# One more pair of key blocks joined in the softmax sums of an attention and MLP block, and two transposes moved behind other matmuls

## The chip, the cores and the metric

The kernel runs on one core of a Trainium2 chip. The metric is the device time of one execution in microseconds (us); the median of three executions of the kernel before is 3200.17 us, from 3200.02 to 3200.99.

## The reference

The input x has 8 sequences of 1024 rows and 512 columns. All arithmetic is float32. A condition vector per sequence gives six modulation vectors: shift, scale and gate for the attention half and for the MLP half.

```
mod = silu(condition) @ Wada + bada          # sh_a, sc_a, gt_a, sh_m, sc_m, gt_m
xm  = layernorm(x, g1, be1) * (1 + sc_a) + sh_a
q, k, v = split(xm @ Wqkv)                   # 16 heads of 32
scores = q k^T * 32**-0.5, masked to k <= q  # causal
x   = x + gt_a * ((softmax(scores) v) @ Wproj + bproj)
xm  = layernorm(x, g2, be2) * (1 + sc_m) + sh_m
x   = x + gt_m * (gelu(xm @ W1 + b1) @ W2 + b2)
```

## The kernel before, in words

Large products are made of three matmuls each, high by high, low by high and high by low part, so that the reduced float32 format of TensorE gives nearly full precision.

The attention is cut into 32 items: one sequence and four heads each. An item is worked through in 20 steps (`score_chunks`), two steps to a slot. A step is one block of 128 keys against a quarter (256) of the queries that may see it; the quarters come last to first, so an item's slots are 0 to 3 (last quarter), 4 to 6, 7 and 8 (second quarter), and 9 (first quarter). Slots 3, 6, 8 and 9 (`DIAG_SLOTS`) hold the diagonal blocks: their first 128 columns are masked after the exponential, and the second of their two blocks is only 128 queries wide.

Two items make a body of 40 steps, s = 0 to 39. There are 16 bodies. In the first 13 (`with_a`) TensorE also does, between the steps, the projections q, k, v of rows further ahead (`a_item`, twelve to a body); in the first 12 of these (`with_ln`) a block of x is also normalised and transposed (`a_turn`, L742, one per 128 columns, four to a body, at the steps of `TURN_AT`: 23, 29, 33, 35). The last three bodies have neither. A stage after them does projection and MLP, and is not touched.

Every engine runs its own list of instructions in order, written out by hand, and waits on semaphores. In a step of a body with `with_a` TensorE (PE) does: the scores of the step in two halves (L838); a transpose of x if the step has one (L756); its share of a projection (L784, L788), unless a new one starts at an odd step, which then comes last (`late`); a piece of the bound on the maximum of a later item, if the step has one (`max_item`, L807; VectorE reduces it at L1345, `max_reduced`); and at odd steps the sums over keys of an earlier slot (`added_sums`, L849), the products with v of the slot before (`values`, L876), and that slot's sums if it is a diagonal one (`diagonal_sums`, L893 and L898). ScalarE does the exponentials (L1097, tile `e`, a ring of 8 steps) and copies each finished projection out of PSUM (L1087), after which `a_turn` may write into that bank, and modulates the transposed block (L1074), after which the next projection may.

The denominators are sums over keys, made by matmuls with a matrix of ones. To have fewer of them GpSimd (POOL) first adds blocks to each other. `SUM_GROUPS[True]` says which slots share one place in the ring `es` of two: before, (0,1,2), (3), (4,5), (6), (7), (8), (9). The first slot of a group is one addition of its two blocks (L1663). A further slot is two: `half_add` (L1639) adds the slot's first block to the place, and then `add` (L1656) adds the second. For a diagonal slot alone, L1663 adds the two halves that are 128 wide, and `diagonal_sums` sums the other 128 columns of `e` itself (L893) and the 128 added ones (L898). It waits for the semaphore `added` between the two, and PE's next instructions are the scores of the step after. POOL also masks the diagonal blocks (L1626), splits q and k into high and low parts (`a_low`, L1617) and takes the power for the normalisation at step 15 (L1610). `values` waits for both masks of its slot.

Of the kernel before, what the change touches and what calls it, by code (L numbers as in the profile page):

```python
# [24 lines left out]
SLOTS = NCH // 2  # L25
# [8 lines left out]
AHEAD = 3  # L34
# [17 lines left out]
TURN_AT, TURN_AFTER = (23, 29, 33, 35), (7, 9, 10, 11)  # L52
# [81 lines left out]
def placed(chunks):  # L134

    return [(*chunk, sum(c[3] for c in chunks[:n])) for n, chunk in enumerate(chunks)]
# [3 lines left out]
DIAG = [c for c, (_, kt, q0, _) in enumerate(CHUNKS) if q0 == P * kt]  # L140


DIAG_SLOTS = [i for i in range(SLOTS) if 2 * i in DIAG]
OTHER_SLOTS = [i for i in range(SLOTS) if i not in DIAG_SLOTS]

SUM_GROUPS = {True: [(0, 1, 2), (3,), (4, 5)] + [(i,) for i in range(6, SLOTS)], False: [(i,) for i in range(SLOTS)]}

HALF_ADDED = [i for g in SUM_GROUPS[True] for i in g[1:]]
HALF_ADDS = len(HALF_ADDED)


def sum_place(h, i, with_a):

    groups = SUM_GROUPS[with_a]
    n = next(n for n, g in enumerate(groups) if i in g)
# [3 lines left out]

SUMS_END = {with_a: [g[-1] for g in groups] for with_a, groups in SUM_GROUPS.items()}  # L160
assert all({groups[-2][-1], groups[-1][-1]} <= set(DIAG_SLOTS) and groups[-1] == (9,) for groups in SUM_GROUPS.values())
LAST_SLOT = {CHUNKS[2 * i][0]: i for i in DIAG_SLOTS}
# [5 lines left out]
def item_at(s):  # L168

    for n, shares in enumerate(A_SHARES):  # L170
        if s < len(shares):
            return n, sum(shares[:s]), sum(shares[:s + 1])
        s -= len(shares)
    return None
# [13 lines left out]
def wait(eng, sem, value):  # L188

    if isinstance(value, int) and value <= 0:  # L190
        return
    eng.wait_ge(sem, value)


def build(nc, x, cond, Wqkv, Wproj, bproj, W1, b1, W2, b2, g1, be1, g2, be2, Wada, bada, out):
# [26 lines left out]
    with ExitStack() as keep:  # L222
        sems = {}

        def sem(name):
            if name not in sems:
                sems[name] = keep.enter_context(nc.semaphore(name))
            return sems[name]
# [477 lines left out]
        def _(pe):  # L706
# [87 lines left out]
            def max_item(u, ahead, n, masks):  # L794

                i = u * 2 + ahead
                if n == 0:  # L800
                    pe.wait_ge(max_loaded[ahead % 2], (u + ahead // 2 + 1) * 32)
                    wait(pe, sem("m_turned"), i)
                wait(pe, sem("max_reduced"), i * NMX + n)
                for qt, part, k0, w, col in placed(MAXES[n][0]):
                    for h in range(GH):
                        rows = slice(HD * h, HD * (h + 1))
                        mm = pe.matmul(psS[:, h, col:col + w], qmx[rows, ahead % 2, qt * P:(qt + 1) * P],  # L807
                                       kmx[rows, ahead % 2, k0:k0 + w], start=True, stop=True,
                                       skip_group_check=True)
                chunks, diag = MAXES[n]  # L810
                if masks and diag is not None:
                    for h in range(GH):
                        at = psS[:, h].rearrange("p (j c) -> p j c", c=P)[:, diag]
                        mm = pe.matmul(at, ident_b[:], mask_b[:].to_broadcast([P, len(chunks) if diag.step else 1, P]),
                                       start=False, stop=True, skip_group_check=True)
                mm.then_inc(sem("max_formed"), 1)
# [25 lines left out]
            def added_sums(u, t, with_a):  # L842

                h, i = divmod(t, SLOTS)
                place, slots, _ = sum_place(h, i, with_a)
                pe.wait_ge(sem("added"), (u * 2 + h) * SLOTS + i + 1)
                past(pe, "pe")
                for hd in range(GH):
                    mm = pe.matmul(psO[HD * hd:HD * (hd + 1), QUART:2 * QUART], ones[:],  # L849
                                   es[:, place, hd, :], start=False, stop=True,  # L850
                                   skip_group_check=True)
                mm.then_inc(sem("summed"), len(slots))
# [65 lines left out]
            def body(u, with_a, with_ln):  # L918
                last = isinstance(u, int) and u == NU - 1
                for s in range(BODY_STEPS):  # L920
                    h, r = divmod(s, NCH)
                    ahead = u == 0 and s == 0
                    if ahead:
                        a_item(AHEAD, *item_at(0), False, with_ln)


                    slot = s % 2 == 1 and not (u == 0 and s == 1)
                    between = s % 2 == 1 and not with_a
                    piece = MAX_AT.get(r)
                    if piece and last and h + piece[0] >= 2:  # L930
                        piece = None
                    sums = slot and s // 2 >= 2 and (s // 2 - 2) % SLOTS in [i for i in SUMS_END[with_a] if i not in DIAG_SLOTS]
                    scores(u, s, 0, with_a)
                    if between and piece:
                        max_item(u, h + piece[0], piece[1], True)
                    elif between and sums:
                        added_sums(u, s // 2 - 2, with_a)
                    scores(u, s, 1, with_a)
                    if with_ln and s in TURN_AT[:-1]:
                        a_turn(u + AHEAD + 1, TURN_AT.index(s), False)  # L940
                    at = item_at(s) if with_a else None
                    late = s % 2 == 1 and at is not None and at[1] == 0
                    if at and not late and not ahead:
                        a_item(u + AHEAD, *at, False, with_ln)
                    if r == MAX_TURN_AT and not (last and h == 1):
                        max_turn(u, h + 1)
                    if piece and not between:
                        max_item(u, h + piece[0], piece[1], not with_a)
                    if slot:
                        t = s // 2  # L950
                        if sums and (piece or not between):
                            added_sums(u, t - 2, with_a)
                        values(u, t - 1)
                        if with_ln and s == TURN_AT[-1]:
                            a_turn(u + AHEAD + 1, A_TURNS - 1, False)
                        diagonal_sums(u, t - 1)
                    if late:
                        a_item(u + AHEAD, *at, False, with_ln)
                    if last and s in FIRST_PROJECT_AT:
                        project(0, 0, FIRST_PROJECT_AT.index(s))  # L960
# [3 lines left out]
            for ia in range(AHEAD):  # L964
                for n in range(A_ITEMS):
# [9 lines left out]
                    if (ia, n) in MAX_ALONE_AT:  # L975
                        ahead, piece = MAX_ALONE_AT[ia, n]
# [10 lines left out]
            for u in range(1, NU - AHEAD - 1):  # L987
                body(u, True, True)
# [597 lines left out]
        def _(pool):  # L1586
# [42 lines left out]
            def half_add(u, t, with_a):  # L1629

                h, i = divmod(t, SLOTS)
                place, slots, _ = sum_place(h, i, with_a)
                if i != slots[0]:
                    if i in DIAG_SLOTS:
                        pool.wait_ge(sem("masked"), (u * 2 + h) * len(DIAG) + 2 * DIAG_SLOTS.index(i) + 1)
                    else:
                        pool.wait_ge(sem("exp_done"), (u * BODY_STEPS + 2 * t + 1) * 2)
                    pool.wait_ge(sem("added"), u * BODY_SLOTS + t)
                    pool.tensor_tensor(es[:, place], es[:, place], e[:, 2 * t % ERING], ALU.add)\  # L1639
                        .then_inc(sem("half_added"), 1)  # L1640
# [35 lines left out]
            def body(u, with_a, with_ln, after_a, pieces):  # L1676
                for s in range(BODY_STEPS):
                    mask(u, s)
                    if s % 2 == 0:
                        half_add(u, s // 2, with_a)  # L1680
                    else:
                        add(u, s // 2, with_a)
                    item = formed(u, s, 1, LOW_LATE, with_a, after_a)
                    if item:
                        a_low(*item)
                    if with_ln and s == LN_AGGR_AT:
                        a_rstd(u + AHEAD + 1)
                    if isinstance(u, int) and u == NU - 1 and s == FIRST_RSTD_AT:
                        rstd_2(0)
                    for part in range(2):  # L1690
                        q = PIECE_AT.get(s - PIECE_LOW_LAG - 2 * part)
                        if q is not None and q < pieces:
                            piece_low(u, q, part)
# [76 lines left out]
```

## Time and profile before

| | us |
|---|---|
| median of three executions | 3200.17 |
| the profiled execution | 3200.24 |
| its span, first to last instruction | 3198.5 |
| PE busy in it | 3129.8 |
| DVE (VectorE) busy | 2351.6 |
| POOL (GpSimd) busy | 1742.8 |
| ACT (ScalarE) busy | 1189.0 |

The span is 1.74 us shorter than the profiled execution's own time. The 13 bodies that the change touches lie between about 173 and 1359 us of the span, and twelve of them take about 92.9 us each; the last stage begins at about 1573 us. All times in rows are from the span's start. Busy time is that in which an engine had an instruction running; a PE that is always busy still waits now and then for a part of a microsecond between rows, which is seen as a jump of the start times.

### The profile page before, as it was taken

How to read it: one execution, taken by the hardware profiler on the slowest of the kernel's cores; microseconds unless marked ns; L12 is line 12 of the kernel's file. 1: busy time of each engine (PE TensorE's matmuls, PEld its weight loads, DVE VectorE, ACT ScalarE, POOL GpSimd, SP SyncE). 2: the span in 40 equal slices, each digit the busy share in tenths (PEclk: the TensorE clock that was granted, in tenths of full speed). 3: DMA queues.
4: the chain of work that ended last, by engine and by line, in shares of the span. 5: the costliest groups of instructions: out<-in, count | busy, mean ns of one | idle time of the engine just before them, and what ended most of it. 6: DMA issues, size and time to landing. Idle time of an engine off the chain costs nothing.

```text
span 3198.5 us, 68318 instructions
## 1 busy us (share of the span) xinstructions
PE 3129.8 (98%) x24936; PEld 2522.6 (79%) x24936; DVE 2351.6 (74%) x2981; ACT 1189.0 (37%) x2354; POOL 1742.8 (54%) x1385
## 2 busy tenths in 40 slices
PE   7999999999999999999899999999999999999999
PEld 5667777776777777766688888989898898988888
DVE  4678887787888777766777767677777777777673
ACT  3355555555555555566521212112121121212211
POOL 3288887888888878888743333233332333333232
PEclk9999999999999999999999999999999999999999
DMA  6666666666656665676612222121322212122120
GB/s 240 215 179 188 177 188 184 176 182 181 195 171 190 185 181 165 193 194 167 167 40 80 48 70 71 47 79 41 77 58 60 79 39 79 54 64 72 46 66 14
DMA packets 304611, 391.85 MB, mean 123 GB/s; under 512 B 24280, under 2 KB 206072, under 8 KB 304432
## 3 DMA queue, kind: packets, MB, share of 16 engines
q1 hardware_dynamic: 292320, 371.86, 40.9%
q10 hardware_dynamic: 12112, 17.42, 1.6%
q8 instruction: 135, 2.21, 0.3%
q14 instruction: 44, 0.36, 0.0%
HBM read 270.66 MB, written 118.00 MB: 122 GB/s over the span
## 4 chain that ended last, share of the span: by engine, by line
PE 89%; DVE 5%; issue 2%; ACT 2%; DMA 1%; POOL 1%; SPq 0%; DVEq 0%; ACTq 0%; POOLq 0%
PE psH L1009 23%; PE psY L1022 22%; PE psA L784 9%; PE psT L838 8%; PE psA L876 8%; PE psP L913 6%; PE psA L788 5%; PE psS L807 4%; DVE mx L1345 2%; PE psA L849 2%; PE psA L756 1%; DVE psS L1341 1%; PE psA L898 1%; ACT e L1097 1%; PE psA L893 1%
## 5 line engine op out<-in xcount | busy, mean ns | idle before, releaser
L1605 POOL TENSOR_TENSOR h_l<-h_full,h_h 128x256 fp32r<-128x256 f32 x512 | 489.8, 957 | 1080.6 <-DVE h_h L1518 1080.6
L1097 ACT ACTIVATE e<-psT 128x512 f32<-128x512 f32 (+1 forms) x1202 | 606.0, 554 | 531.5 <-PE psT L838 529.0
L1345 DVE TENSOR_REDUCE mx<-psS 128x4 f32<-128x2048 f32 (+3 forms) x384 | 665.8, 1755 | 116.7 <-PE psS L807 79.5
L1220 ACT ACTIVATE h_full<-psH,b1c 128x256 f32<-128x256 f32 x512 | 242.9, 475 | 1226.9 <-PE psH L1009 1226.9
L1009 PE MATMUL psH<-a_h,w1p_h 128*128 128x256 f32 x2048 | 575.2, 281 | 2.2 <-DVE a_l L1513 2.2
L1009 PE MATMUL psH<-a_l,w1p_h 128*128 128x256 f32 x2048 | 577.0, 282 | 0.0
L1009 PE MATMUL psH<-a_h,w1p_l 128*128 128x256 f32 x2048 | 576.7, 282 | 0.0
L1663 POOL TENSOR_TENSOR es<-e 128x512 f32<-128x512 f32 (+1 forms) x242 | 446.3, 1845 | 168.6 <-ACT e L1097 83.9
L1518 DVE CAST h_h<-h_full 128x256 fp32r<-128x256 f32 x512 | 180.8, 353 | 404.1 <-ACT h_full L1220 401.2
L838 PEld LDWEIGHTS psT<-qst,kst 97*128 97x128 f32 x2404 | 349.1, 189 | 114.4 <-issue 70.8
L838 PE MATMUL psT<-qst,kst 97*128 97x256 f32 (+1 forms) x2404 | 410.4, 290 | 4.5 <-ACT e L1097 3.3
L1009 PEld LDWEIGHTS psH<-a_h,w1p_h 128*128 128x128 f32 x2048 | 388.3, 190 | 24.6 <-DVE a_l L1513 2.6
L1009 PEld LDWEIGHTS psH<-a_l,w1p_h 128*128 128x128 f32 x2048 | 388.9, 190 | 21.7
L1022 PE MATMUL psY<-w_l,h_h 128*128 128x512 f32 x1024 | 404.6, 395 | 0.0
L1022 PE MATMUL psY<-w_h,h_h 128*128 128x512 f32 x1024 | 402.0, 393 | 2.5 <-DVE tmp L1525 2.5
L1022 PE MATMUL psY<-w_h,h_l 128*128 128x512 f32 x1024 | 402.6, 393 | 0.0
L1009 PEld LDWEIGHTS psH<-a_h,w1p_l 128*128 128x128 f32 x2048 | 389.5, 190 | 0.0
L876 PE MATMUL psA<-e,vst 128*32 128x256 f32 (+1 forms) x5120 | 313.7, 362 | 9.3 <-ACT o_sb L1105 7.3
L1431 DVE RECIPROCAL oin<-oin 128x256 f32<-128x256 f32 x128 | 221.9, 1739 | 47.0 <-DMA oin<-sums 47.0
L876 PEld LDWEIGHTS psA<-e,vst 128*32 128x32 f32 x5120 | 146.0, 109 | 122.4 <-issue 45.0
L1617 POOL TENSOR_TENSOR qk_hl<-qk_hl 128x512 fp32r<-128x512 f32 x128 | 166.8, 1304 | 122.1 <-ACT qk_hl L1180 68.8
L1495 DVE STREAM_TRANSPOSE a_full<-xc 32x256 f32<-32x256 f32 x512 | 223.3, 436 | 9.4
(118 smaller groups left out, 5213.5 us busy)
## 6 DMA issues: line engine op xcount, KB each, us to landing
qk_split<-qk_hl SPq DMA_DIRECT2D x128, 512.0 KB, 3.6
kst<-qk_split SPq DMA_DIRECT2D x128, 256.0 KB, 3.9
qst<-qk_split SPq DMA_DIRECT2D x128, 256.0 KB, 4.2
xin<-in_x_dram SPq DMA_DIRECT2D x64, 256.0 KB, 3.5
values<-vout ACTq DMA_DIRECT2D x64, 256.0 KB, 3.3
kmx<-qk_split SPq DMA_DIRECT2D x32, 512.0 KB, 4.7
qmx<-qk_split SPq DMA_DIRECT2D x32, 512.0 KB, 5.7
kst<-qk_split SPq DMA_DIRECT2D x128, 128.0 KB, 3.8
```

Source lines behind the costliest of these rows:

```text
L784: mm = pe.matmul(psA[:, bank, :], w[:, k, m * P:(m + 1) * P], a[:, k, :], **ends)
L838: mm = pe.matmul(bank[:, d, 0:w], kst[0:97, hd, key_cols(kt, h)], qst[0:97, q0 // HALF, hd, q0 % HALF:q0 % HALF + w], start=True, stop=Tru ...
L876: mm = pe.matmul(psO[HD * hd:HD * (hd + 1), c:c + w], vst[:, h, kt, HD * hd:HD * (hd + 1)], e[:, (2 * t + d) % ERING, hd, 0:w], start=(kt ...
L1009: mm = pe.matmul(psH[:, m % 4, 0:RA], w[:, k, m * P:(m + 1) * P], a[par][:, k, :], start=(n == 0), stop=(n == 3 * KT - 1))
L1022: mm = pe.matmul(psY[:, r, :], a[:, m % 4, r * P:(r + 1) * P], w[:, w2_at(m), :], start=(m == 0 and n == 0), stop=(m == FT - 1 and n == 2) ...
L1097: act.activation(e[:, s % ERING, 2 * hp:2 * hp + 2, 0:w], score_bank(s, hp, with_a)[:, :, 0:w], ACT.Exp, scale=SCALE).then_inc(sem("exp_do ...
L1220: act.activation(h_full[:, m % 4, :], psH[:, m % 4, 0:RA], ACT.Gelu, bias=b1c[:, m:m + 1])\
L1345: reduce = dve.tensor_reduce(mx[:, part, :, qt], psS[:, :, col:col + w], AX_X, ALU.max)
L1431: dve.reciprocal(oin[:, 1, k], oin[:, 1, k]).then_inc(sem("sums_inverted"), 1)
L1495: t = dve.transpose(cols[:, :, :, a], rows[:, :, :, b])
L1605: return pool.tensor_tensor(dst, full, high.bitcast(F32), ALU.subtract)
L1663: pool.tensor_tensor(to, first, second, ALU.add).then_inc(sem("added"), 1)
```

## The change

One more group of two slots: (7) and (8) become (7,8). Slot 8 is diagonal, so three rules change with it. `half_add` of a diagonal slot is issued at the odd step, after both masks of the slot and just ahead of its `add`, and waits for both masks. `added_sums` no longer sums slot 7, and `diagonal_sums` of slot 8 takes all 256 columns from `es` after the `added` of slot 8, with no matmul on `e`. The lists without projections (the last three bodies) stay as they are. On PE, the transposes at steps 23 and 29, where a piece of the maximum falls too, are issued behind that piece; those at 33 and 35 stay.

```diff
-SUM_GROUPS = {True: [(0, 1, 2), (3,), (4, 5)] + [(i,) for i in range(6, SLOTS)], False: [(i,) for i in range(SLOTS)]}
+SUM_GROUPS = {True: [(0, 1, 2), (3,), (4, 5), (6,), (7, 8), (9,)], False: [(i,) for i in range(SLOTS)]}
@@ TensorE, body
-                    if with_ln and s in TURN_AT[:-1]:
+                    turn = with_ln and s in TURN_AT[:-1]
+                    if turn and not piece:
                         a_turn(u + AHEAD + 1, TURN_AT.index(s), False)
...
                     if piece and not between:
                         max_item(u, h + piece[0], piece[1], not with_a)
+                    if turn and piece:
+                        a_turn(u + AHEAD + 1, TURN_AT.index(s), False)
@@ GpSimd, half_add
-                        pool.wait_ge(sem("masked"), (u * 2 + h) * len(DIAG) + 2 * DIAG_SLOTS.index(i) + 1)
+                        pool.wait_ge(sem("masked"), (u * 2 + h) * len(DIAG) + 2 * DIAG_SLOTS.index(i) + 2)
@@ GpSimd, body
                     mask(u, s)
-                    if s % 2 == 0:
+                    if (s % 2 == 1) == (s // 2 % SLOTS in DIAG_SLOTS):
                         half_add(u, s // 2, with_a)
-                    else:
+                    if s % 2 == 1:
                         add(u, s // 2, with_a)
```

## Rows read from the trace of the kernel before

**Rows 1.** The page: busy time by engine.
```profile
PE 3129.8 (98%) x24936; PEld 2522.6 (79%) x24936; DVE 2351.6 (74%) x2981; ACT 1189.0 (37%) x2354; POOL 1742.8 (54%) x1385
```
**Rows 2.** Twelve bodies: length, busy PE, PEld, DVE, ACT, POOL, then PEclk, DMA.
```profile
184.51:1298.79 1114.28, 1099.26 (x10970) 784.69 (x10969) 902.40 (x801) 630.60 (x1248) 915.98 (x613) 1.00 0.63 182
```
**Rows 3.** Timeline of PE, step 19 of a body: start, length, what.
```profile
659.03 0.64 PE L849 MATMUL psA<-es,ones 128*32 128x256 f32 x8
659.48 0.83 PE L876 MATMUL psA<-e,vst 128*32 128x256 f32 x16
660.13 0.40 PE L893 MATMUL psA<-e,ones 128*32 128x128 f32 x8
660.64 0.43 PE L898 MATMUL psA<-es,ones 128*32 128x128 f32 x8
661.00 0.74 PE L838 MATMUL psT<-qst,kst 97*128 97x256 f32 x4
661.58 0.40 PE L784 MATMUL psA<-xm_h,wqkv_h 128*128 128x512 f32 x1
```
**Rows 4.** Timeline of POOL, steps 11 to 20 of the same body.
```profile
641.96 1.28 POOL L1617 TENSOR_TENSOR qk_hl<-qk_hl 128x512 fp32r<-128x512 f32 x1 [1.07 <-DVE qk_hl L1329]
643.20 2.39 POOL L1639 TENSOR_TENSOR es<-es,e 128x1024 f32<-128x1024 f32 x1
645.67 2.39 POOL L1656 TENSOR_TENSOR es<-es,e 128x1024 f32<-128x1024 f32 x1
...
659.22 1.28 POOL L1663 TENSOR_TENSOR es<-e 128x512 f32<-128x512 f32 x1 [0.26 <-POOL e L1626]
...
661.94 1.76 POOL L1663 TENSOR_TENSOR es<-e 128x512 f32<-128x512 f32 x1 [0.26 <-POOL e L1626]
```
**Rows 5.** Timeline of DVE beside it.
```profile
661.88 0.68 DVE L1329 TENSOR_TENSOR qk_hl<-qk_hl 128x512 fp32r<-128x512 f32 x1
```
**Rows 6.** Timeline of POOL and PE, steps 37 to 39 of the same body.
```profile
704.50 1.29 POOL L1663 TENSOR_TENSOR es<-e 128x512 f32<-128x512 f32 x1 [0.26 <-POOL e L1626]
...
708.60 0.40 PE L893 MATMUL psA<-e,ones 128*32 128x128 f32 x8
708.82 0.40 PE L898 MATMUL psA<-es,ones 128*32 128x128 f32 x8
709.15 0.74 PE L838 MATMUL psT<-qst,kst 97*128 97x256 f32 x4
```
**Rows 7.** Timeline of PE at steps 23 and 29, and of DVE.
```profile
665.41 2.36 DVE L1345 TENSOR_REDUCE mx<-psS 128x4 f32<-128x512 f32 x2
...
667.19 0.64 PE L838 MATMUL psT<-qst,kst 97*128 97x256 f32 x4
668.19 0.63 PE L756 MATMUL psA<-ident,xin 128*128 128x128 f32 x4 [0.36 <-ACT qk_hl L1087]
...
681.44 0.64 PE L838 MATMUL psT<-qst,kst 97*128 97x256 f32 x4
682.35 0.66 PE L756 MATMUL psA<-ident,xin 128*128 128x128 f32 x4 [0.27 <-ACT vout L1087]
```
**Rows 8.** Timeline of POOL and PE, step 17 to 19 of the thirteenth body.
```profile
1307.80 1.28 POOL L1663 TENSOR_TENSOR es<-e 128x512 f32<-128x512 f32 x1 [0.21 <-ACT e L1097]
...
1310.03 0.40 PE L893 MATMUL psA<-e,ones 128*32 128x128 f32 x8
```
**Rows 9.** Timeline of PE: two gaps, with their length in brackets.
```profile
1567.48 0.44 PE L838 MATMUL psT<-qst,kst 97*128 97x128 f32 x2 [1.93 <-ACT e L1097]
...
1637.14 0.77 PE L1022 MATMUL psY<-w_h,h_h 128*128 128x512 f32 x1 [2.47 <-DVE tmp L1525]
```
**Rows 10.** Stretches behind those gaps, and one with shorter gaps; columns as Rows 2.
```profile
1568.42:1575.24 6.82, 5.63 (x68) 4.01 (x59) 6.79 (x6) 3.56 (x5) 6.42 (x4) 0.50 0.14 30
1636.69:1640.10 3.41, 2.96 (x8) 2.41 (x9) 2.30 (x5) 0.00 (x0) 1.24 (x2) 0.50 0.10 41
1528.50:1535.00 6.50, 3.90 (x51) 2.87 (x47) 6.43 (x4) 3.30 (x7) 5.59 (x5) 1.00 1.13 230
```

## The prediction

> **What bounds the kernel now.** I read the page first: PE is busy for 98% of the span [rows 1]. Then the stretch of the bodies that change: in twelve of them, 1114.28 us or 92.86 us each, PE is busy for 1099.26 us at a granted clock of 1.00, POOL for 915.98 us, which is 82%, DVE for 81% [rows 2]. So PE sets the time, and every microsecond taken from its stream counts. But POOL is a close second: it has 16.5 us of slack in a body on average, and an average says nothing of where. So I went to the timelines of PE and POOL at the one place where PE waits for what POOL adds, `diagonal_sums` of slot 8 at steps 19 and 39.
>
> Step 19, the first item of a body [rows 3]: L849 (the sums of slot 7) starts at 659.03, the products with v at 659.48, L893 at 660.13, L898 at 660.64, the next scores at 661.00. At step 39 L893 takes 0.22 us of the stream and L898 0.33, until the next scores at 709.15 [rows 6]. Here the two last 0.87 us, so PE already waits about 0.3 us. The reader sees for what in POOL's rows: the addition of slot 8 runs 659.22 to 660.50, and L898 starts 0.14 us after its end [rows 4]. I find it in all twelve bodies with normalisation, one of which stands in the rows. POOL is at work there without a pause but those of its own hand-overs since 641.96, when it waited 1.07 us for DVE. At step 39 it is early: the addition of slot 8 ends at 705.79, and PE asks for it only at 708.82 [rows 6].
>
> **The change part by part.** The working is for one body of twelve, in the body of these rows.
>
> PE, sums. Per item, L849 of slot 7 goes: 659.48 - 659.03 = 0.45 us. L893 and L898 of slot 8, 0.55 us with the switch back to scores [rows 6], become four matmuls of 256 columns from `es`. The same form, L849, takes 0.45 us, and the switch adds 0.11 us (0.33 for L898 against 0.22 for L893), so 0.56 us: no change. Taken alone, with 26 items, this saves 26 x 0.45 = 11.7 us.
>
> POOL, the new half addition. Each of 26 items gets one more addition of 128x1024, 2.39 us by L1639 at 643.20 [rows 4]. It adds 2 x 2.39 us to POOL's 76.3 us of 92.86, which as a share of time still fits. But it stands directly ahead of the addition for which PE waits, and PE can do none of its new sums before that. What is queued behind PE's wait is the scores of step 20, and behind these ScalarE's exponentials, POOL's masks, and everything else.
>
> At step 19: both masks done, the half addition starts where the addition did, at 659.22, and ends at 661.61. The hand-over to the second one is 0.08 us (643.20 + 2.39 against 645.67), and 1.28 us more give 662.97. The addition of slot 9 at 661.94 took 1.76 us and not 1.28, with a DVE operation on two SBUF tiles (L1329) at 661.88 to 662.56 beside it [rows 4, 5]. DVE has work of its own there (the rest of the normalisation, L1296, behind this step's reduction), so the second addition may end at 663.45 instead. With 0.14 us PE goes on at 663.11 or 663.59, and reaches the next scores 0.56 us later: 663.67 or 664.15 against 661.00. PE asks 0.45 us earlier, at 659.68, so it stands for 3.4 to 3.9 us. The net loss is 2.67 to 3.15 us, and contains the saving of L849. I take 2.9, as the middle of two ends that are close. Nothing gives it back: the masks and the addition of slot 9 move by the same 2.4 to 2.9 us as PE's step 21 which needs them.
>
> The Trainium skill bears on the 0.48 us between these ends: its page "SBUF — State Buffer", section "SBUF: two separate sides", says that DVE operations with two SBUF inputs and GpSimd's reads take a shared port pair by an exclusive lock, and the later one blocks in full. The 1.76 us of the row agree. By that rule the upper end is due in each body, 3.15 x 12 = 37.8 us; by the undisturbed length 2.67 x 12 = 32.0 us.
>
> At step 39: the half addition runs 704.50 to 706.89, the addition from 706.97 to 708.25, or to 708.73 if disturbed. PE, which now asks at 708.60 - 0.45 = 708.15, goes on at 708.39 or 708.87 and is at the scores at 708.95 or 709.43, against 709.15: between 0.20 us won and 0.28 us lost. I take 0. POOL has idle time on both sides there.
>
> PE, the two transposes. At step 23 the scores start at 667.19 and the transpose at 668.19, 1.00 us later; a group of the same shape without a wait is followed after 0.58 us (661.00 to 661.58) [rows 3], so some 0.42 us are a wait for ScalarE's copy out of that bank. At step 29 it is 0.91 us, so 0.33 us [rows 7]. With the piece of the maximum ahead, which takes about 0.45 us, that wait lies under work. What is late next: at step 23 the piece needs the reduction that ends at 667.77, and PE is there at 667.77, so about 0.1 us stays; and the projection that starts last in the step needs ScalarE to have modulated the block, for which the products with v (1.0 us) are left as cover. I take 0.32 and 0.34, together 0.66 us per body, 7.9 us in twelve. The bounds are 0 (all of it comes back as a wait for the modulated block) and 0.75. No DMA or queue is moved, and the reordering on POOL issues the same masks.
>
> The thirteenth body has no normalisation, so POOL is earlier: half addition from 1307.80, second done at 1311.55, PE on at 1311.69 where it would have asked at 1309.58 [rows 8], scores at 1312.25 against 1310.03 + 0.55 = 1310.58. That is 1.7 us lost, and its second item, with POOL early, wins about 0.45: 1.2 us.
>
> PE's clock. This is the cost that no part of the code names. In the bodies, where PE never stands for long, the granted clock is 1.00 [rows 2]. Behind a gap of 1.93 us at 1567.48 it was 0.50 (1.2 of 2.4 GHz) for 6.82 us, and behind one of 2.47 us at 1637.14 for 3.41 us. A stretch with only 3.90 us of PE work in 6.50, but in shorter gaps, kept 1.00 [rows 9, 10]. The new stall of 3.4 to 3.9 us in every body is longer than both, so I expect a half-rate stretch of 3.41 us at each. PE's work in it costs double, so it costs up to 3.41 / 2 = 1.7 us, less when a part of it lies still in the stall. Bounds are 0 and 3.41 (a stretch of 6.82). I take 1.3, nearer to the single stretch: 12 x 1.3 = 15.6 us.
>
> The page "TensorE: Matmul & The Clock Gate" of the Trainium skill, section "HAM oscillation — how this bites in real kernels", describes such a loop, where a wait in every tile drops the clock every time. By that rule each body pays, as here; a reader who doubts it takes the rival below.
>
> **The sum.** 12 x 2.9 = 34.8, 12 x 0 at step 39, minus 7.9, plus 1.2, plus 15.6: 43.7 us slower. The profiled execution took 3200.24 us, its span of 3198.5 and 1.74 around it, and the median is 3200.17, so both give 3243.9; I say 3243.
>
> **Rivals.**
> A. The stall comes, the clock stays. For it: no row shows a regular stall of this kind, and PE is dense on both sides of it. Against it: both gaps above. 34.8 - 7.9 + 1.2 = 28.1, so 3228.
> B. The clock falls for 6.82 us at each stall, as behind the 1.93 us gap; there a second gap of 0.87 us followed soon, which is missing here. 28.1 + 12 x 3.0 = 64, so 3264.
> C. Faster: PE's saving is kept, since POOL reaches slot 8 earlier than now. Its place is the wait at 641.96, 1.07 us for DVE. It decides from the point where POOL is ahead by more than the stall, 3.4 us; a gain of 11.7 + 7.9 = 19.6 us, so 3181. For it: DVE's and POOL's idle times are not fixed, and a slower PE leaves them ahead. Against it: 1.07 us is all the pause that POOL has in the 18 us before, so it would have to lose three times as much work.
> D. POOL regains that 1.07 us and the clock holds: (2.9 - 1.07) x 12 - 7.9 + 1.2 = 15, so 3215. With a bit more it comes near no change.
>
> That the change doesn't do what it says is not likely: the matmuls of slot 7 go by the list itself.
>
> **Chances.** Forecast 0.48, A 0.24, B 0.10, C 0.09, D 0.09. The range of 8 in 10 is 3213 to 3264: it leaves out C, most of B's upper side and the low end of D. Differences of 0.2%, 6.4 us, are about what a measurement of this kernel can tell from none. Faster is C, 0.09; of D about a third would end within 0.2%, 0.03; slower is 0.88.
>
> **What would show it.** In the profile after, PE's own rows: 26 groups of L849 gone and 26 of L893. At step 19 a gap on PE of 3 to 4 us in twelve bodies ahead of L898, put down to POOL L1656, and L1639 rows up by 26. At step 39 a gap under 0.8 us. At steps 23 and 29 the idle time before L756 put down to ScalarE gone (it stays at step 33), and none new before the projections. PEclk under 1.00 behind each stall. Bodies of 92.9 us become about 96.4. It is wrong if step 19 shows a stall under 1 us (then C), wrong in size if PEclk stays at 1.00 (A), and wrong in its sign if PE's sums wait for nothing.

## The result: 3.0% slower, and what the profile after shows

The changed kernel takes 3297.43 us (median of five executions, 3292.07 to 3300.78) against 3200.17 us: a ratio of 1.0301, 95% interval 1.0289 to 1.0313. The forecast was 3243 with a range of 3213 to 3264. The direction was right, but the loss of 97 us is more than twice the 43 forecast.

The page after: TensorE (PE) is busy for 96% of a longer span with 416 fewer instructions, POOL (GpSimd) has 26 more. The second line gives the shares of the chain of work that ended last; before, PE had 89% of it, DVE (VectorE) 5%, issue 2% and POOL 1%.

```profile
PE 3161.7 (96%) x24520; PEld 2534.5 (77%) x24520; DVE 2381.3 (72%) x2981; ACT 1189.1 (36%) x2354; POOL 1806.7 (55%) x1411
...
PE 81%; DVE 7%; issue 5%; POOL 4%; ACT 1%; DMA 1%; DVEq 0%; SPq 0%; ACTq 0%; POOLq 0%
```

The same twelve bodies as in [rows 2] (columns: length, busy time of PE, its weight loads, DVE, ACT and POOL, then PEclk, the granted clock) grow from 1114.28 to 1210.08 us, by 95.8, which is nearly all of the loss. PE's granted clock in them is 0.96 and no longer 1.00.

```profile
184.40:1394.48 1210.08, 1130.00 (x10585) 795.55 (x10584) 935.54 (x801) 630.92 (x1248) 976.80 (x638) 0.96 0.58 168
```

PE's waits in the whole trace (what waited, for what: us in total, times, longest) now begin with two lines. The second is the one that the prediction is about. The first, for DVE's reductions of the maximum, is in no part of it.

```profile
PE psS L807 <- DVE mx L1348: 43.6, 32, 2.1
PE psA L898 <- POOL es L1659: 35.9, 13, 3.2
```

Lines behind L940 are numbered three higher than before, so L1348 is the reduction L1345, L1323 and L1325 the split of x (L1320, L1322), L1642 the half addition (L1639), L1659 and L1666 the additions (L1656, L1663).

**By step.** PE's step lengths, from the start of a step's scores to that of the next, averaged over ten bodies in the middle. "Quiet" are the 40 steps from step 19 at 799.27 us to the next step 19 at 896.82, the "quiet body", in which the clock never fell.

| step | before | after | quiet body |
|---|---|---|---|
| 19 | 3.19 | 5.76 | 5.19 |
| 20 | 1.96 | 3.12 | 1.95 |
| 21 | 2.28 | 2.55 | 2.28 |
| 23 | 3.58 | 3.23 | 3.24 |
| 29 | 3.97 | 3.64 | 3.64 |
| 39 | 2.87 | 2.60 | 2.58 |
| 1 | 2.28 | 3.63 | 3.64 |
| 2 | 1.95 | 2.21 | 2.21 |
| 3 | 2.64 | 5.38 | 4.75 |
| 4 | 2.30 | 2.59 | 2.33 |
| all 40 | 92.89 | 100.41 | 97.6 |

The quiet body is 4.7 us longer than one before: 2.0 at step 19, 0.7 won at 23 and 29, 0.3 won at 39, 3.7 lost at steps 1 to 3. The mean over the twelve bodies is (1210.08 - 1114.28) / 12 = 8.0 us. The other 3.3 us per body are 39 us in all. About 4 us of these are a longer stall: in six of the twelve bodies PE waits 3.2 us at step 19 and not 2.56, since POOL reaches slot 8 half a microsecond later in PE's time. These are the six before which the clock did not fall behind step 3; a PE slowed there finding POOL further on fits this. The rest, some 35 us, is PE's work at half clock: in the twelve bodies the clock falls 17 times, ten times behind step 19 and seven times behind step 3, for 85 us together.

Step 19 of the quiet body, POOL, PE and one row of DVE; it answers to [rows 3, 4]. The second addition ends at 803.74, and L898 starts 0.15 us later, after 2.56 us of idle time.

```profile
800.05 2.35 POOL L1642 TENSOR_TENSOR es<-es,e 128x1024 f32<-128x1024 f32 x1 [0.16 <-POOL e L1629]
...
800.60 2.29 DVE L1348 TENSOR_REDUCE mx<-psS 128x4 f32<-128x2048 f32 x1 [0.43 <-PE psS L807]
...
802.48 1.26 POOL L1659 TENSOR_TENSOR es<-es,e 128x512 f32<-128x512 f32 x1
...
803.89 0.64 PE L898 MATMUL psA<-es,ones 128*32 128x256 f32 x8 [2.56 <-POOL es L1659]
804.46 0.73 PE L838 MATMUL psT<-qst,kst 97*128 97x256 f32 x4
```

Steps 37 to 3 of the same stretch, DVE, POOL and PE; it answers to [rows 6].

```profile
846.89 2.40 POOL L1642 TENSOR_TENSOR es<-es,e 128x1024 f32<-128x1024 f32 x1 [0.16 <-POOL e L1629]
848.44 1.13 DVE L1323 CAST xm_h<-xin 128x512 fp32r<-128x512 f32 x1
849.37 1.34 POOL L1659 TENSOR_TENSOR es<-es,e 128x512 f32<-128x512 f32 x1
849.61 1.65 DVE L1325 TENSOR_TENSOR xm_l<-xin,xm_h 128x512 fp32r<-128x512 f32 x1
849.63 0.50 PE L807 MATMUL psS<-kmx,qmx 32*128 32x512 f32 x4
...
850.86 0.64 PE L898 MATMUL psA<-es,ones 128*32 128x256 f32 x8
...
852.99 2.28 DVE L1348 TENSOR_REDUCE mx<-psS 128x4 f32<-128x2048 f32 x1
855.19 2.65 POOL L1666 TENSOR_TENSOR es<-e 128x1024 f32<-128x1024 f32 x1 [0.98 <-ACT e L1100]
...
855.33 0.56 PE L807 MATMUL psS<-kmx,qmx 32*128 32x128 f32 x8 [1.29 <-DVE mx L1348]
855.63 2.76 DVE L1325 TENSOR_TENSOR xm_l<-xin,xm_h 128x512 fp32r<-128x512 f32 x1
...
858.32 1.22 DVE L1344 TENSOR_TENSOR psS<-psS,mask_q 128x1024 f32<-128x1024 f32 x1
...
861.98 0.51 PE L807 MATMUL psS<-kmx,qmx 32*128 32x256 f32 x8 [2.09 <-DVE mx L1348]
```

PE's sums (L898) are in time there, as forecast. But look at DVE. The same stretch before, at steps 37 to 1, with the PE and POOL rows that the comparison needs:

```profile
705.87 0.42 DVE L1320 CAST xm_h<-xin 128x512 fp32r<-128x512 f32 x1
706.33 0.69 DVE L1322 TENSOR_TENSOR xm_l<-xin,xm_h 128x512 fp32r<-128x512 f32 x1
...
707.05 0.51 PE L807 MATMUL psS<-kmx,qmx 32*128 32x512 f32 x4
...
708.75 2.28 DVE L1345 TENSOR_REDUCE mx<-psS 128x4 f32<-128x2048 f32 x1
...
711.39 0.69 DVE L1322 TENSOR_TENSOR xm_l<-xin,xm_h 128x512 fp32r<-128x512 f32 x1
712.30 1.23 DVE L1341 TENSOR_TENSOR psS<-psS,mask_q 128x1024 f32<-128x1024 f32 x1 [0.21 <-PE psS L807]
712.91 2.40 POOL L1663 TENSOR_TENSOR es<-e 128x1024 f32<-128x1024 f32 x1 [2.94 <-ACT e L1097]
```

The cast takes 1.13 us and not 0.42: it ends 0.28 us behind POOL's half addition, in the middle of which it began. The subtraction takes 1.65 and not 0.69, and ends 0.55 us behind POOL's second addition. So step 39's reduction starts 3.36 us after its matmuls (L807, 849.63) in place of 1.70 (707.05). The last subtraction (855.63), which before was through (712.08) when POOL began on the next item (712.91), now begins under that addition and takes 2.76 us. The next masking and reduction start late, and PE waits for them at steps 1 and 3.

The clock (PEclk, third number from the right), in a stretch of the quiet body and two of other bodies. Behind the stall of 3.20 us that ends at 601.61 it is 0.50, in the quiet body behind 2.56 us it stays 1.00, and at 662 it falls behind the wait at step 3.

```profile
803.50:806.00 2.50, 2.11 (x17) 1.55 (x18) 2.34 (x3) 0.92 (x2) 2.24 (x4) 1.00 0.94 210
601.20:604.60 3.40, 3.00 (x15) 2.02 (x16) 1.58 (x2) 1.07 (x3) 3.14 (x4) 0.50 0.96 218
662.00:669.00 7.00, 6.57 (x43) 4.57 (x44) 4.56 (x5) 1.35 (x3) 3.77 (x3) 0.76 0.12 38
```

### The profile page after: what moved, and what is told of

Read it like the earlier page. It is cut to its first block, busy times and chain, and to the rows that moved or that the text cites. A ratio compares the mean times of both kernels' runs of the same rounds, so it can differ in the third digit from the quotient of the medians.

```text
span 3295.4 us, 67490 instructions
## 1 busy us (share of the span) xinstructions
PE 3161.7 (96%) x24520; PEld 2534.5 (77%) x24520; DVE 2381.3 (72%) x2981; ACT 1189.1 (36%) x2354; POOL 1806.7 (55%) x1411
## 4 chain that ended last, share of the span: by engine, by line
PE 81%; DVE 7%; issue 5%; POOL 4%; ACT 1%; DMA 1%; DVEq 0%; SPq 0%; ACTq 0%; POOLq 0%
PE psH L1012 22%; PE psY L1025 21%; PE psA L784 8%; PE psT L838 7%; PE psA L876 6%; PE psP L913 5%; PE psA L788 5%; PE psS L807 3%; DVE mx L1348 3%; PE psA L849 1%; DVE xm_h L1323 1%; POOL es L1666 1%; DVE psS L1344 1%; PE psA L756 1%; POOL es L1642 1%
## 5 line engine op out<-in xcount | busy, mean ns | idle before, releaser
L1348 DVE TENSOR_REDUCE mx<-psS 128x4 f32<-128x2048 f32 (+3 forms) x384 | 666.1, 1756 | 128.8 <-PE psS L807 92.0
L1666 POOL TENSOR_TENSOR es<-e 128x1024 f32<-128x1024 f32 (+1 forms) x216 | 409.5, 1896 | 155.9 <-ACT e L1100 78.1
L838 PEld LDWEIGHTS psT<-qst,kst 97*128 97x128 f32 x2404 | 357.9, 194 | 123.8 <-issue 78.9
L838 PE MATMUL psT<-qst,kst 97*128 97x256 f32 (+1 forms) x2404 | 419.2, 294 | 3.5 <-ACT e L1100 3.3
L1642 POOL TENSOR_TENSOR es<-es,e 128x1024 f32<-128x1024 f32 x104 | 247.5, 2380 | 26.9 <-ACT e L1100 22.0
L1344 DVE TENSOR_TENSOR psS<-psS,mask_q 128x1024 f32<-128x1024 f32 (+1 forms) x135 | 137.1, 1016 | 148.9 <-PE psS L807 148.6
```

Of the source, the lines that this page charges most:

```text
L838: mm = pe.matmul(bank[:, d, 0:w], kst[0:97, hd, key_cols(kt, h)], qst[0:97, q0 // HALF, hd, q0 % HALF:q0 % HALF + w], start=True, stop=Tru ...
L1348: reduce = dve.tensor_reduce(mx[:, part, :, qt], psS[:, :, col:col + w], AX_X, ALU.max)
L1666: pool.tensor_tensor(to, first, second, ALU.add).then_inc(sem("added"), 1)
```

## The experiments

All are compared with the kernel before on the same chip (medians 3201.07, 3201.52 and 3201.76 in the three groups). Theory: two separate losses, POOL late for PE at step 19, and DVE held up beside POOL's half addition at step 37, for which PE pays at steps 1 to 4. Rival: one loss, the second a shadow of the first or of the moved transposes.

### The transposes alone, and the join alone

```diff
 # turns_only: the changed kernel with
-SUM_GROUPS = {True: [(0, 1, 2), (3,), (4, 5), (6,), (7, 8), (9,)], ...
+SUM_GROUPS = {True: [(0, 1, 2), (3,), (4, 5)] + [(i,) for i in range(6, SLOTS)], ...
 # join_only: the changed kernel with the transposes as before
-                    turn = with_ln and s in TURN_AT[:-1]
-                    if turn and not piece:
+                    if with_ln and s in TURN_AT[:-1]:
                         a_turn(u + AHEAD + 1, TURN_AT.index(s), False)
...
-                    if turn and piece:
-                        a_turn(u + AHEAD + 1, TURN_AT.index(s), False)
```

> The changed kernel with the sum groups of before: only the two transposes at steps 23 and 29 are moved. Theory (each part is priced by its own steps): steps 23 and 29 get shorter by 0.34 us each in twelve bodies, nothing else changes: 3200.2 - 8.1 = 3192. Rival (the moved transposes disturb VectorE's reductions and cause the new waits at steps 1 and 3): over 3220.

> The join (7,8) and POOL's new order alone, the transposes where they were before. Theory: the whole loss is the join's, and the transposes had won 8 us of it: 3297.4 + 8 = 3305, with the waits of TensorE for VectorE's reduction at steps 1 and 3 still there. Rival (these waits need the moved transposes): 3297.4 - 12 x 3.7 + 8 = 3261.

Measured: 3192.32 us, ratio 0.9973 (0.9963 to 0.9983), and 3305.75, ratio 1.0322 (1.0306 to 1.0338). The steps 23 and 29 are 3.22 and 3.63 us in the first, 3.57 and 3.97 in the second; steps 1 and 3 are 2.28 and 2.65 in the first, 3.63 and 5.24 in the second. So the two parts add up, the transposes win 8 to 9 us, and the join owns the whole loss.

### The half addition made tiny: in the first item, in the second, in both

```diff
-pool.tensor_tensor(es[:, place], es[:, place], e[:, 2 * t % ERING], ALU.add)
+w = 1 if i in DIAG_SLOTS and h == 0 else QUART      # small17; h == 1 in small37; no condition on h in small_both
+to, part = es[:, place, :, 0:w], e[:, 2 * t % ERING, :, 0:w]
+pool.tensor_tensor(to, to, part, ALU.add)
```

> The changed kernel, but the new half addition of slot 8 in the first item of each body (step 17) adds 4 columns in place of 1024; it leaves out that part of the sums. Theory (two separate causes, POOL late at step 19 and VectorE held up behind step 37): the stall at step 19 goes with its clock losses, which are 2.3 to 3.2 us, 0.3 of a wait that was there before, and 1.3 to 2.3 us at half clock, about 4.9 us in twelve bodies; the waits at steps 1 and 3 stay: 3297.4 - 59 = 3239. Rival (steps 1 and 3 are late because step 19 was): near 3190.

> The changed kernel, but the new half addition of slot 8 in the second item of each body (step 37) adds 4 columns in place of 1024; it leaves out that part of the sums. Theory (POOL's half addition at step 37 holds up VectorE's split of x and so its reductions, for which TensorE waits at steps 1 and 3): 3.7 us at steps 1 to 3 go and some 1.3 us of half clock behind them, 12 x 5 = 60: 3237, with VectorE's casts at step 37 back at 0.42 us. Rival (steps 1 and 3 are late because the body's other stall shifts the engines against each other): no change, 3297.

> The changed kernel with the new half additions of slot 8 of both items cut to 4 columns; it leaves out that part of the sums. Theory (all the loss is the time that POOL's two new additions take): TensorE keeps its fewer matmuls. At step 39 that wins 0.45 us in 13 bodies, at step 19 nothing, since the second addition still ends where it did: 3192 (the transposes alone) - 6 = 3186. Rival (a part of the loss is the new order of masks and additions, or the waits that it adds): over 3200.

Measured: 3244.80 us (ratio 1.0139, 1.0124 to 1.0155), 3247.90 (1.0145, 1.0129 to 1.0160) and 3194.76 (0.9980, 0.9970 to 0.9989). By step, in us:

| step | before | after | small17 | small37 |
|---|---|---|---|---|
| 19 | 3.19 | 5.76 | 3.36 | 6.14 |
| 20 | 1.96 | 3.12 | 1.97 | 3.28 |
| 1 | 2.28 | 3.63 | 3.64 | 2.28 |
| 3 | 2.64 | 5.38 | 5.10 | 2.78 |

Each cures its own steps and leaves the other's, which refutes the rival. The two cures are worth 53 and 50 us, and both together 103, which leaves nothing of the loss. They fell short of what was expected of them by 6 and 11 us. For small37 the reason can be read: with no fall behind step 3 any more, the stall at step 19 is 3.2 us in all twelve bodies and no longer 2.56 in six. In PE's waits the line for the reductions is as large as ever with the first cure, and the line for POOL with the second, where that for the reductions is down to 3.2 us (small17, then small37; the line numbers of POOL's additions differ a little from kernel to kernel):

```profile
PE psS L807 <- DVE mx L1348: 43.7, 32, 2.1
PE psA L898 <- POOL es L1661: 8.2, 12, 0.9
```

```profile
PE psA L898 <- POOL es L1661: 40.3, 13, 3.2
```

small_both missed its number by 9 us: with no real half addition at all the join is no better than the transposes alone (3192.32). Its step 39 wins 0.44 us as worked out, but step 19 is 3.57 against 3.17 us. Half of that is the tiny operation and its hand-over ahead of the addition that PE waits for; half is that all 256 columns of the sums now stand behind the wait (0.57 us to the next scores in place of 0.36). So the join's whole prize is smaller than 11.7 us before it costs POOL anything.

### The sums of the first item behind the next step's work

```diff
                         values(u, t - 1)
-                        diagonal_sums(u, t - 1)
+                        if not (with_a and (t - 1) % SLOTS == 8 and (t - 1) // SLOTS in (0,)):
+                            diagonal_sums(u, t - 1)
+                    if r == 0 and with_a and h:
+                        diagonal_sums(u, s // 2 - 2)
```

> The changed kernel, but the sums of slot 8 of a body's first item are issued on TensorE behind the scores and the projection's share of step 20, not ahead of them. POOL does the same work. Theory (TensorE stands only because its stream is in order): 1.9 us of step 20 go under the stall, what is left of it is some 2 us, and the half clock behind it goes too: 3297 - 13 x 3.0 = 3258, steps 1 to 3 as before. Rival (the clock falls behind 2 us as well): 3275. If the scores of step 20 were held up by something else than the order: 3297.

Measured: 3259.57 us, ratio 1.0185 (1.0168 to 1.0202). Steps 19, 20 and 21 are 2.02, 3.49 and 3.13 us, 8.64 in place of 11.43; steps 1 and 3 are as in the changed kernel. The wait before L898 is 0.55 us in six bodies, one of which is shown, and 1.15 in the others, and a second one has come at the next slot, whose addition is late as well:

```profile
491.74 0.64 PE L898 MATMUL psA<-es,ones 128*32 128x256 f32 x8 [0.55 <-POOL es L1662]
...
495.08 0.43 PE L898 MATMUL psA<-es,ones 128*32 128x128 f32 x8 [0.50 <-POOL es L1669]
```

So the stall was PE's order as forecast, but POOL's 2.4 us don't vanish: they are handed on to step 21.

### VectorE's reduction ahead of its split at step 39

```diff
-if with_ln and s in SPLIT_AT:
+if with_ln and s in SPLIT_AT and s != 39:
     a_split(u + AHEAD + 1, SPLIT_AT[s])
 if r in MAX_AT:
     ...
+if with_ln and s == 39:
+    a_split(u + AHEAD + 1, SPLIT_AT[s])
```

> The changed kernel, but VectorE does step 39's reduction of the maximum ahead of step 39's split of x, not behind it. Theory (TensorE's waits at steps 1 and 3 are VectorE's queue, in which the splits are held up beside POOL's additions): the wait of 1.35 us at step 1 goes, that of step 3 shrinks by some 0.5 to 1 us but stays in part, since the split at step 0 is held up by POOL's addition of the next item: 3297 - 12 x 2.2 = 3271. Rival (the reductions are late because POOL is, or because their input is): 3297.

Measured: 3298.45 us, ratio 1.0307 (1.0290 to 1.0324): nothing won, a miss. Step 1 is 2.27 us, so the wait there did go. But step 2 is 3.33 in place of 2.21 and step 3 6.30 in place of 5.38. The split that now comes later is itself waited for, by the projection at step 2, and the subtraction of step 0 is still under POOL's addition for 2.75 us:

```profile
755.90 2.75 DVE L1325 TENSOR_TENSOR xm_l<-xin,xm_h 128x512 fp32r<-128x512 f32 x1
...
758.70 0.50 PE L784 MATMUL psA<-xm_h,wqkv_h 128*128 128x512 f32 x1 [1.08 <-DVE xm_l L1325]
...
762.24 0.80 PE L807 MATMUL psS<-kmx,qmx 32*128 32x256 f32 x8 [2.10 <-DVE mx L1348]
```

It is consistent with the theory that DVE as a whole is late, not one item in its queue; the order only chooses which of PE's waits is paid. The clock has a part in the result too: it falls in each of the twelve bodies behind step 19 and behind step 3, 102 us at half clock in place of 85.

### The half addition in four parts

```diff
+if i in DIAG_SLOTS:                    # quarters; and h == 1 in quarters37
+    for hd in range(GH):
+        part = pool.tensor_tensor(es[:, place, hd], es[:, place, hd], e[:, 2 * t % ERING, hd], ALU.add)
+    part.then_inc(sem("half_added"), 1)
+    return
```

> The changed kernel, with each new half addition of slot 8 issued as four additions of 128x256, one per head, in place of one of 128x1024; the same result. Theory (a VectorE operation on two SBUF tiles or a cast waits until the POOL instruction that runs beside it ends): VectorE's splits at steps 37 to 39 wait 0.6 us at most in place of 1 us, so steps 1 and 3 get shorter by 1 to 2 us in all, but POOL now waits for VectorE in between and the stall at step 19 may grow by 0.3 us: 3297 - 12 x 1 = 3285. Rival (the hold-up isn't by instruction): 3297 or above, with the casts at step 37 still at 1.2 us.

> The changed kernel, with the new half addition of slot 8 in four parts of 128x256 in the second item of a body only. Theory (VectorE is held up by instruction, and steps 1 to 4 are late for that alone): steps 1 to 4 lose 4.7 us of the 5.0 that the change added there, step 39 gets 0.9 us longer, step 19 stays: 3297 - 12 x 3.8 = 3252. Rival (quartering at step 17 was what helped): 3290 or more.

Measured: 3277.89 us (ratio 1.0242, 1.0225 to 1.0259), and 3271.31 (1.0219, 1.0204 to 1.0235). In both, steps 1 to 4 are 2.61, 1.96, 2.93 and 2.30 us, 9.8 in place of 13.8. So the same amount of POOL work at the same place, in shorter instructions, takes four of the 4.6 us away. In quarters37:

```profile
736.03 3.00 POOL L1644 TENSOR_TENSOR es<-es,e 128x256 f32<-128x256 f32 x4 [0.16 <-POOL e L1629]
737.50 0.94 DVE L1323 CAST xm_h<-xin 128x512 fp32r<-128x512 f32 x1
738.47 1.11 DVE L1325 TENSOR_TENSOR xm_l<-xin,xm_h 128x512 fp32r<-128x512 f32 x1
...
740.85 0.64 PE L898 MATMUL psA<-es,ones 128*32 128x256 f32 x8 [0.87 <-POOL es L1664]
...
744.59 0.69 DVE L1325 TENSOR_TENSOR xm_l<-xin,xm_h 128x512 fp32r<-128x512 f32 x1
745.17 2.39 POOL L1671 TENSOR_TENSOR es<-e 128x1024 f32<-128x1024 f32 x1 [1.11 <-ACT e L1100]
```

The subtraction at 744.59 starts ahead of POOL's next long addition (745.17) again and keeps its 0.69 us. POOL pays: the four parts last 3.00 us and not 2.40. In the first item (quarters) four parts take 2.77 us, with a DVE reduction from PSUM beside them; the other 0.2 us fit a wait for DVE in turn, which isn't shown. PE's sums at step 39 wait 0.87 us. I had expected 3252 for quarters37 and got 3271. Its steps 19 to 21 are 12.4 us and not 11.4. The clock falls behind step 19 in every one of the twelve bodies, and in ten of twelve of the changed kernel. Step 19 itself grows, at an unchanged operation, for the reason seen in small37: no clock falls behind step 3 any more, POOL is not ahead at step 19 in any body, and the stall is 3.2 us in all twelve. The traces of join_only, small17, late20, reduce_first and join_late agree: POOL is half a microsecond ahead at step 19 in the bodies where the clock fell behind step 3 just before, and in no other.

### Both remedies, and the transposes with late sums

join_late is quarters37 with the sums of slot 8 behind the next step's work in both items; turns_late is turns_only with the edit of late20.

> The join with both remedies: the half addition of the second item in four parts, and the sums of slot 8 behind the work of the next step (20, and 0 of the next body) in both items; the same result. Against the kernel before, per body: transposes 0.7 won, steps 19 to 21 1.2 lost as measured with the sums behind step 20, step 39 and 0 about 0.45 won, steps 1 to 3 some 0.6 lost: 3200 + 12 x 0.7 = 3208. If the two remedies disturb each other: over 3225. If it beats the transposes alone, it is under 3192.

> The kernel before with the two transposes moved, and the sums of slot 8 of a body's first item behind the work of step 20; no join. Theory: the 0.3 us that TensorE waits for POOL at step 19 without any join goes as well: 3192.3 - 12 x 0.3 = 3189. Rival (ScalarE's copy of the finished quarter comes later, and step 21 waits for it): 3192 or more.

Measured: 3231.80 us (ratio 1.0089, 1.0075 to 1.0102) and 3194.15 (0.9976, 0.9967 to 0.9986). The remedies disturb each other: with the sums in step 0, step 0 is 2.63 us in place of 1.97 and steps 1 and 3 are 3.41 and 3.23. The clock in the bodies is back at 1.00 but for one fall of 3.4 us, so these 30 us are waits nearly alone. turns_late wins nothing over turns_only: steps 19 to 21 are 7.54 against 7.42 us. Its small wait for POOL went, and as much came back. I haven't tried to find at what; ScalarE's copy, which the rival named, fits but isn't shown.

The best version found is turns_only, 0.27% faster than the kernel before.

## Why the prediction was wrong

- PE bounds, POOL close behind: right. All the loss comes from POOL's two new half additions per body; with them made tiny, nothing of it is left (small_both).
- The stall at step 19: right. Worked out was an end of the second addition 5.15 to 5.63 us after the step's start; it is 4.47 in the quiet body and 5.20 in another. The quiet body loses 2.0 us, against 2.67 forecast at least, as POOL was half a microsecond earlier in its list than in the body I read. POOL is early like that in six bodies; in the other six step 19 loses 3.2 us. Steps 19 to 21 as they are, clock included, lose 4.0 us, against 2.9 + 1.3. In the thirteenth body step 19 loses 1.0 us, against 1.7.
- The transposes: 0.68 us per body against 0.66, and 8.8 us in turns_only against 7.9.
- Step 39 for PE: 0.27 won, just outside the bounds of 0.20 won and 0.28 lost, and near the 0 that the sum took.
- **The step that failed** is the conclusion drawn there: "between 0.20 us won and 0.28 us lost. I take 0. POOL has idle time on both sides there." PE and POOL were all I looked at. At step 19 I had used a row in which POOL and DVE hold each other up, but only for what it costs POOL. At step 37 the same hold-up the other way round costs DVE 0.71 us at the cast and 0.96 at the subtraction. DVE has a reduction for PE queued behind these, and a third operation that just missed POOL's next addition. The term that was missing is 3.7 us per body at steps 1 to 3 in the quiet body, 45 us in twelve; small37 gives it with its clock losses as 50 us. The cover that I had not priced was 0.8 us: the time, just behind [rows 6], between the end of DVE's last subtraction (712.08) and POOL's next addition (712.91).
- The clock: I said 1.3 us per body, bounds 0 and 3.41; it is about 2.9, an estimate from the step lengths (35 us in twelve bodies). The mechanism is right, the size is not: most bodies have two long waits, not one, and eight of the 17 falls lasted 6.83 us. Without the second wait (small37, steps 19 to 21 still slow) the half-rate stretches in these bodies sum to 58 us, in the changed kernel to 85 us, without the first (small17) to 17 us. The rule of the Trainium skill cited for it, page "TensorE: Matmul & The Clock Gate", section "HAM oscillation — how this bites in real kernels", fits ten of the twelve stalls at step 19, but not the one in the quiet body, whose 2.56 us wait left the clock at 1.00. That wait is shorter than those of the loop that the page describes, so it doesn't speak against the page either.
- The rivals: B, a longer fall of the clock (3264), was the nearest, and its upper side was cut off by the range. It too lacks the second wait. C, a gain, didn't come, but its premise is seen: a PE slowed at step 3 finds POOL half a microsecond ahead at step 19.

The Trainium skill's rule on the shared port pair ("SBUF — State Buffer", "SBUF: two separate sides") is the one that I used on half of its range. It names both sides as the one that may block; DVE's cast and subtraction ending 0.28 and 0.55 us behind POOL's instruction agree with it, and so does the cure by shorter instructions. It says so of a DVE operation with two SBUF inputs, or of one in a mode that uses both port pairs; that the cast runs in such a mode isn't shown here.

## What to carry to other kernels

When work is added to an engine that shares something with another, price it for the other's queue too: find which of its instructions will run beside the new ones, what stands behind them, and which consumer that feeds. Look for how narrowly an operation now misses the next long one of the neighbour, as that margin, and not the idle time of the engine with the new work, is what covers it. Two edits of one change are best read by step lengths: here one was worth 8 us and was hidden under a loss of 105.

## What was not expected of the hardware

- A VectorE cast of 0.42 us took 1.13 us, and a two-input operation of 0.69 us took 1.65 and 2.76, beside GpSimd additions; a reduction from PSUM beside such an addition (800.60 and 800.05) kept its 2.29 us.
- Cutting one GpSimd addition of 2.40 us into four made it 3.00 us, and the kernel 26 us faster (quarters37).
- TensorE's clock: waits of 2.56 us were followed by 1.2 GHz in some bodies and not in others, and the stretches were 3.41 or 6.83 us long. A fall behind step 3 went with a stall of 2.56 us in place of 3.2 at the next step 19.
